# Front: mask products right behind their scores; slots 3 to 13: GpSimd's long operations behind the zero tests, moments ahead of the first matrix rows

## The chip, the cores and the metric

The kernel runs on one core of a Trainium2 chip. The metric is the device time of one execution in microseconds. The engines have short names in the views: PE is TensorE, DVE is VectorE, ACT is ScalarE, POOL is GpSimd, SP is SyncE, whose queue issues nearly all DMAs.

## The reference

```
def attention(decoder_output, encoder_output, mask):
    q = decoder_output @ wq_w + wq_b; k = encoder_output @ wk_w + wk_b; v = encoder_output @ wv_w + wv_b
    # 16 heads of 32
    score = einsum('bhqd,bhkd->bhqk', q, k) / sqrt(32)
    score = score * mask
    score = where(score == 0, -1e9, score)
    context = einsum('bhqk,bhkd->bhqd', softmax(score), v)
    return context @ wo_w + wo_b

def ffn(x):
    return real(ifft(fft(x) @ (w_freq_real + i w_freq_imag))) + bias

x = x + attention(layernorm(x), ctx_1024, mask)     # x is (2, 2048, 512), ctx_1024 is (2, 128, 512)
x = x + ffn(layernorm(x))
```

## The kernel before

The 4096 tokens are cut into 16 chunks of 256. A chunk takes four slots, one for each group of four heads, so there are 64 slots with scores (s = 4 * chunk + group), and the loop over v runs from 2 to 79, as later stages of a chunk trail its scores. Every engine has its own program, written out by hand in the order of the slots, and engines meet at semaphores alone. On each engine instructions start in program order, so one that waits holds everything behind it.

The stages of slot s, with the names of the code:

- PE `scores(s, t)` writes two score tiles into `scores`; it stands in the slot before (v = s - 1) and waits until the mask product of the slot before has read them.
- DVE `mask_mul(s)` (L917) multiplies the scores by the mask row scaled with the first layernorm's factor (`ms`), from PSUM into `zs`. DVE `zero_to_neg(s)` (L924, the zero test, which raises `eq_done`) turns exact zeros into the large negative value, in place in SBUF. DVE `least(s)` (L929) takes the minimum of each row and head.
- POOL `bias(s)` (L1151) scales that minimum into `nbias`, ACT `exps(s, t)` (L726) exponentiates, PE `turn(s, f)` transposes (L623), ACT `copy_pt` (L735) moves the result to SBUF, PE `weigh(m)` (L637) multiplies by the values for two slots at a time, and POOL `spread`, PE "R" and DVE `ctx_norm` normalise it.
- "WO" is the output projection with its residual, "FF" the folded frequency matrix, "Q" and "QQ" are query projections: "Q" of chunks 0 and 1 by quarters in the front, "QQ" of chunk c by halves, each 24 matmuls. `plan()` places the halves of chunk 2 in slots 2 and 4, those of chunk 3 in slots 5 and 6, and from slot 7 on one half in each odd slot.

PE's fp32-like products are made of fp16 pairs, a high and a low part. ACT `split_hi(c)` writes the high part `xth` of the transposed input, POOL `split_lo(c)` (L1102) the low part `xtl` and raises `p_l1`. A query projection of chunk c >= 1 waits for both:

```
                elif kind == "QQ":
                    pe.wait_ge(p_l1, c)
```

`xtl` and `xth` have two buffers, and the next `load_xt` on SP's queue waits for `p_l1` too. POOL's other long work is `fold(n)` (L1178, twelve additions that fold the frequency matrix; "U", which makes the matrix with "M", waits for six and then twelve of them), `low_o` (low part of the output weights), `add_bo` and `add_bf` (biases onto the residual, L1111 and L1137), `ctx_lo` (L1164), and `scale_mask(c)` (L1144). `stat_cols(c)` (L1088 to L1098) turns the moments of chunk c, which DVE makes with `stats1` and `mean1` (L955, L960), into columns that PE's "ST" transposes.

Before slot 2 stands the front, written out call by call on each engine. On PE it ends with S0 (scores of slot 0), W1, Q(0,2), Q(0,3), S1, ST1, Q(1,0), Q(1,1), S2, Q(1,2), Q(1,3). `scores(s)` of chunk 0 waits for `tt_done`, which `mask_mul` raises, and for the query quarter's low part.

In the loop POOL waits for `eq_done` of the same slot from slot VS = 9 on, ahead of its long operations. Below that slot it has no such wait.

Of the kernel before, what the change touches and what calls it, by code (L numbers as in the profile page):

```python
# [119 lines left out]
def bo_slot(c):  # L120

    return c + 7 if c < 3 else 4 * c + 3 if c < 13 else 2 * c + 27


def build(nc, x, xt, ctx_in, mask, wq, bq, wk, bk, wv, bv, wo, bo, lparts, tables, bf, eye, sums, pick, places, heads, out):
# [3 lines left out]
    with ExitStack() as stack:  # L129
# [213 lines left out]
        def _(sp):  # L343
# [87 lines left out]
            for v in range(V0, V1):  # L431
# [9 lines left out]
                if r == 0 and 5 <= c + 4 < NC:  # L441
                    load_xt(c + 4)
# [217 lines left out]
        def _(act):  # L660
# [172 lines left out]
        def _(dve):  # L833
# [190 lines left out]
            lo(at["Q", 1, 1])
            zero_to_neg(1)
            least(1)
            lo(at["Q", 1, 2])
            mask_mul(V0)
            lo(at["Q", 1, 3])
            for v in range(V0, V1):  # L1030
# [25 lines left out]
                for n in mids:  # L1056
                    if fills[n][0] == "M":
                        lo(n)
# [18 lines left out]
        def _(pool):  # L1077
# [150 lines left out]
            fold(3)
            for v in range(V0, V1):
# [3 lines left out]
                if v == VP:  # L1233
                    fold(7)
# [29 lines left out]
                if r < 2 and 0 <= c - 3 < NC:  # L1264
                    add_bf(c - 3, r)
# [16 lines left out]
                for a in (3, 4):  # L1282
                    if lo_slot(a) == v:
                        split_lo(a)
                if v == 3:
                    fold(6)
# [102 lines left out]
```

## Time and profile before

| | |
|---|---|
| median of 3 runs | 449.24 us (449.22 to 450.0) |
| profiled execution, its own time | 449.74 us |
| its span | 448.0 us |
| PE busy | 431.6 us, 96% |
| DVE busy | 402.7 us, 90% |
| ACT busy | 368.2 us, 82% |
| POOL busy | 361.0 us, 81% |

The span is what the profiler saw from the first to the last record; 1.74 us of the profiled execution's time lie around it. The busy time of an engine counts its data instructions alone. A row of the timeline gives start and duration in us, engine, source line, operation, and what it writes and reads. A bracket at its end is the idle time ahead of it and who ended that.

### The profile page before, as it was taken

To read this page: it belongs to the slowest core of one execution; us is meant where nothing else is said; L and a number is where in the kernel's file an instruction comes from. 1 tells how busy PE (TensorE), PEld (TensorE's weight loads), DVE (VectorE), ACT (ScalarE), POOL (GpSimd) and SP (SyncE) were. 2 spreads that over 40 slices of the span, in tenths; PEclk is the share of its full clock that TensorE was granted. 3 is DMA by queue.
4 is the path that set the end of the run, shared out by engine and by line. 5 is a ranking of instruction groups with operands and counts; after the bars stand their busy time and mean duration, and the time that the engine had idled before them with its cause. 6 is when DMAs were issued, how large, how long until landed. Compare 5 with 4: busy or idle time off the path is not lost.

```text
span 448.0 us, 10895 instructions
## 1 busy us (share of the span) xinstructions
PE 431.6 (96%) x3496; PEld 298.1 (67%) x3496; DVE 402.7 (90%) x532; ACT 368.2 (82%) x1342; POOL 361.0 (81%) x482
## 2 busy tenths in 40 slices
PE   7989999998899999999999999999999999989997
PEld 6877678786576666666776667666666765555444
DVE  3799899899999999999999999999999899999353
ACT  1648989799889989898989998989999899999620
POOL 5769997995779898989989898989898778755763
PEclk9999999999999999999999999999999999999999
DMA  8999754404434454545456554555442324431243
GB/s 271 397 385 221 249 190 113 129 1 119 113 105 93 136 126 119 148 117 139 128 139 137 129 145 113 121 104 130 137 95 64 97 75 96 78 83 35 61 115 121
DMA packets 85286, 60.15 MB, mean 134 GB/s; under 512 B 40141, under 2 KB 72813, under 8 KB 84718
## 3 DMA queue, kind: packets, MB, share of 16 engines
q1 hardware_dynamic: 84508, 59.29, 49.0%
q8 instruction: 29, 0.48, 0.5%
q14 instruction: 27, 0.22, 0.2%
q10 hardware_dynamic: 722, 0.17, 0.2%
HBM read 29.33 MB, written 8.39 MB: 84 GB/s over the span
## 4 chain that ended last, share of the span: by engine, by line
PE 68%; DVE 14%; issue 6%; ACT 5%; POOL 5%; DMA 1%; DVEq 0%; SPq 0%; POOLq 0%; ACTq 0%
PE bank L464 27%; PE bank L469 18%; PE bank L623 8%; PE bank L637 5%; DVE zs L924 4%; PE scores L609 4%; ACT zs L726 3%; DVE zs L917 3%; PE bank L570 2%; POOL cl L1164 2%; PE bank L551 1%; DVE nmin L929 1%; DMA cxs<-in_ctx 1%; PE scores L469 1%; DVE x L902 1%
## 5 line engine op out<-in xcount | busy, mean ns | idle before, releaser
L726 ACT ACTIVATE zs<-zs,nbias 128x128 f32<-128x128 f32 x512 | 199.5, 395 | 18.0 <-POOL nbias L1151 17.3
L726 ACT ACTIVATION_READ_ACCUMULATOR zs<-zs,nbias 128x1 f32 x512 | 98.4, 192 | 0.0
L924 DVE SCALAR_TENSOR_TENSOR zs<-zs 128x1024 f32<-128x1024 f32 x64 | 92.1, 1439 | 1.1
L929 DVE TENSOR_REDUCE nmin<-zs 128x8 f32<-128x1024 f32 x64 | 78.1, 1220 | 2.1
L917 DVE TENSOR_TENSOR zs<-scores,ms 128x1024 f32<-128x1024 f32 x64 | 78.0, 1219 | 0.1
L735 ACT COPY pt<-bank 128x512 f32<-128x512 f32 x128 | 67.8, 580 | 7.4 <-PE bank L623 7.3
L623 PE MATMUL bank<-ident,zs 128*128 128x128 f32 x512 | 67.0, 274 | 1.9 <-ACT zs L726 1.9
L1111 POOL TENSOR_TENSOR xs<-xs,bob 128x512 f32<-128x512 f32 (+1 forms) x41 | 42.8, 1048 | 24.7 <-DVE zs L924 21.6
L623 PEld LDWEIGHTS bank<-ident,zs 128*128 128x128 f32 x512 | 57.5, 140 | 5.6 <-ACT zs L726 4.5
L469 PE MATMUL bank<-xth,wqh 128*128 128x256 f16 x224 | 61.2, 273 | 0.0
L469 PE MATMUL bank<-xth,wql 128*128 128x256 f16 x224 | 61.1, 273 | 0.0
L469 PE MATMUL bank<-xtl,wqh 128*128 128x256 f16 x224 | 61.1, 273 | 0.0
L464 PE MATMUL bank<-woh,ch 128*128 128x512 f16 x128 | 48.5, 379 | 2.9 <-POOL cl L1164 2.1
L464 PE MATMUL bank<-woh,cl 128*128 128x512 f16 x128 | 48.5, 379 | 0.0
L464 PE MATMUL bank<-wol,ch 128*128 128x512 f16 x128 | 48.5, 379 | 0.0
L464 PE MATMUL bank<-mh,x1h 128*128 128x512 f16 x120 | 45.5, 379 | 0.0
L464 PE MATMUL bank<-ml,x1h 128*128 128x512 f16 x120 | 45.5, 379 | 0.0
L464 PE MATMUL bank<-mh,x1l 128*128 128x512 f16 x120 | 45.5, 379 | 0.0
L609 PEld LDWEIGHTS scores<-ks,qs 102*128 102x128 f16 (+1 forms) x480 | 31.7, 97 | 16.6 <-DVE zs L917 3.6
L1137 POOL TENSOR_TENSOR x<-x,bfb 128x512 f32<-128x512 f32 x32 | 40.8, 1276 | 0.0
L1164 POOL TENSOR_TENSOR cl<-cn,ch 128x512 f16<-128x512 f32 x32 | 38.1, 1190 | 3.3 <-ACT ch L749 3.3
L1158 POOL COPY rzb<-rz 128x512 f32<-128x512 f32 x32 | 40.6, 1268 | 0.2 <-DVE rz L935 0.2
(125 smaller groups left out, 910.8 us busy)
## 6 DMA issues: line engine op xcount, KB each, us to landing
xs<-in_x SPq DMA_DIRECT2D x16, 512.0 KB, 4.7
xtr<-in_xt SPq DMA_DIRECT2D x16, 512.0 KB, 4.4
out<-x SPq DMA_DIRECT2D x31, 256.0 KB, 2.5
qs<-qh SPq DMA_DIRECT2D x120, 64.0 KB
lp<-in_lparts SPq DMA_DIRECT2D x4, 1024.0 KB, 9.9
qs<-ql SPq DMA_DIRECT2D x60, 64.0 KB
ms<-in_mask SPq DMA_DIRECT2D x16, 128.0 KB, 2.4
wks<-in_wk SPq DMA_DIRECT2D x2, 512.0 KB, 6.8
```

The lines of the kernel that those rows point to most:

```text
L464: last = pe.matmul(o, a, b, start=(i == 0), stop=(i == len(mm) - 1))
L469: last = pe.matmul(o, a, b, start=(first and i == 0), stop=(i == len(pairs) - 1))
L609: last = pe.matmul(A[:, n % 2, 128 * j:128 * j + 128], qs[c % 2][0:rows, g, j, 128 * t:128 * t + 128], ks[0:rows, g, j, c // (NC // NB), : ...
L623: last = pe.transpose(PB[f][:, a:a + 128], zs[:, s % NZ, t, 2 * f + i, :], ident[:])
L726: last = act.activation(z, z, ACT.Exp, bias=nbias[:, s % 4, i:i + 1], scale=-NEG, accum_out=zsum[:, s % 4, i:i + 1])
L735: act.copy(pt[:, s % 2, 2 * f:2 * f + 2, :], PB[f][:]).then_inc(pt_copied, 1)
L917: dve.tensor_tensor(zs[:, s % NZ], A[:].rearrange("p t (h k) -> p t h k", h=4), ms[:, c % NM].unsqueeze(2).broadcast_to([128, 2, 4, KEYS]) ...
L924: dve.scalar_tensor_tensor(out=z, in0=z, scalar=0.0, in1=z, op0=ALU.is_equal, op1=ALU.subtract).then_inc(eq_done, 1)
L929: dve.tensor_reduce(nmin[:, s % 4, :], zs[:, s % NZ].rearrange("p t h k -> p (t h) k"), AX.X, ALU.min).then_inc(mn_done, 1)
L1111: i = pool.tensor_tensor(z, z, bob[:, n], ALU.add)
L1137: pool.tensor_tensor(z, z, bfb[:], ALU.add).then_inc(p_x1b, 1)
L1164: pool.tensor_tensor(cl[:, c % 2, 2 * h:2 * h + 2, :], cn[:], ch[:, c % 2, 2 * h:2 * h + 2, :], ALU.subtract).then_inc(p_cl, 1)
```

## The change

No instruction's size changes. What changes is the order on DVE and POOL, one pair of calls on ACT, and the place of one load on SP.

- Front, DVE: `mask_mul(0)` and `mask_mul(1)` move up; the moments of chunks 1 and 2 are pulled apart and stand around other work. Front, ACT: `exps(1, 0)` ahead of the copy of Q(1,3). Front, POOL: `bias(0)` between folds 0 and 1, then a wait for the second zero test, fold 2, `bias(1)`, and only then `split_lo(2)`.
- POOL's wait for the zero test starts at VP = 4. Folds 6 to 11 get new places (6 to 9 in slot 4, 10 and 11 in slot 5).
- `split_lo(3)` moves from slot 3 to slot 6, and `split_lo(4)` from slot 6 to slot 7, in halves around `bias`. `scale_mask(2)` moves from slot 4 to the end of slot 6, `add_bo(2, .)` from slot 9 to 10, `add_bf(0, 0)` from the middle of slot 12 to its end.
- The moments of chunk 6 move from slots 10 and 11 into slot 8, and the DVE part of "M" 0 goes behind them. `load_xt(5)` moves from slot 4 to slot 6 of SP's program.

```
--- before.py
+++ after.py
@@ -18,7 +18,6 @@
 NC = NB * S // CH
 NS = 4 * NC
 V0, V1 = 2, NS + 16
-VS = 9
 VP = 4
 VQ = 13
 LAST = ("FF", NC - 1, 1)
@@ -102,7 +101,7 @@
 
 
 def stats_slot(c, t):
-    return 4 if c == 4 else 4 * (c - 4) + 2 + t
+    return 4 if c == 4 else 8 if c == 6 else 4 * (c - 4) + 2 + t
 
 
 def small_slot(c):
@@ -113,13 +112,9 @@
     return 5 if c == 4 else 4 * (c - 3)
 
 
-def lo_slot(c):
-    return 3 if c == 3 else 6
-
-
 def bo_slot(c):
 
-    return c + 7 if c < 3 else 4 * c + 3 if c < 13 else 2 * c + 27
+    return c + 7 if c < 2 else 10 if c == 2 else 4 * c + 3 if c < 13 else 2 * c + 27
 
 
 def build(nc, x, xt, ctx_in, mask, wq, bq, wk, bk, wv, bv, wo, bo, lparts, tables, bf, eye, sums, pick, places, heads, out):
@@ -438,7 +433,9 @@
                     load_mask(c + 2)
                 if r == 0 and 0 <= c - 4 < NC:
                     store(c - 4, 1)
-                if r == 0 and 5 <= c + 4 < NC:
+                if v == 6:
+                    load_xt(5)
+                if r == 0 and 6 <= c + 4 < NC:
                     load_xt(c + 4)
                 if r == 3 and 0 <= c - 2 < NC - 1:
                     turn_x1n(c - 2, 0)
@@ -782,8 +779,8 @@
             hi(at["Q", 1, 1])
             exps(0, 1)
             hi(at["Q", 1, 2])
+            exps(1, 0)
             hi(at["Q", 1, 3])
-            exps(1, 0)
             exps(1, 1)
             for v in range(V0, V1):
                 c, r = divmod(v, 4)
@@ -1009,22 +1006,28 @@
             lo(at["Q", 0, 0])
             low_q(1)
             lo(at["Q", 0, 1])
-            moments(1)
+            mask_mul(0)
+            stats1(1, 0)
             lo(at["W1", 1])
-            mask_mul(0)
+            stats1(1, 1)
+            mean1(1, 0)
+            mean1(1, 1)
             spread_k(1)
+            zero_to_neg(0)
+            least(0)
+            mask_mul(1)
             lo(at["Q", 0, 2])
-            zero_to_neg(0)
             lo(at["Q", 0, 3])
-            least(0)
+            zero_to_neg(1)
             lo(at["ST", 1])
-            mask_mul(1)
+            least(1)
             lo(at["Q", 1, 0])
-            moments(2)
             lo(at["Q", 1, 1])
-            zero_to_neg(1)
-            least(1)
+            stats1(2, 0)
+            stats1(2, 1)
             lo(at["Q", 1, 2])
+            mean1(2, 0)
+            mean1(2, 1)
             mask_mul(V0)
             lo(at["Q", 1, 3])
             for v in range(V0, V1):
@@ -1054,7 +1057,7 @@
                 if 0 <= v - 9 < 4:
                     low_m(v - 9)
                 for n in mids:
-                    if fills[n][0] == "M":
+                    if fills[n][0] == "M" and v > 8:
                         lo(n)
                 tasks = []
                 tasks += [(stats1, mean1, a, t) for a in range(4, NC) for t in range(2) if stats_slot(a, t) == v]
@@ -1068,6 +1071,8 @@
                     recip((v - 3) // 2)
                 for _, mean, *ct in tasks:
                     mean(*ct)
+                if v == 8:
+                    lo(at["M", 0])
                 if c - 2 == NC - 1 and r < 2:
                     last_lo2(r)
                 if v == 2:
@@ -1218,20 +1223,19 @@
             split_lo(1)
             stat_cols(1)
             fold(0)
+            bias(0)
             fold(1)
-            bias(0)
+            pool.wait_ge(eq_done, 2)
+            fold(2)
+            bias(1)
             split_lo(2)
             stat_cols(2)
-            bias(1)
             scale_mask(1)
-            fold(2)
             fold(3)
             for v in range(V0, V1):
                 c, r = divmod(v, 4)
                 if v == 8:
                     constant_row()
-                if v == VP:
-                    fold(7)
                 for a in range(5, NC):
                     if small_slot(a) == v:
                         stat_cols(a)
@@ -1239,8 +1243,16 @@
                     rstd2(c - 2, 0)
                 if r == 2 and 0 <= c - 2 < NC:
                     rstd2(c - 2, 1)
-                if VS <= v < NS:
+                if VP <= v < NS:
                     pool.wait_ge(eq_done, v + 1)
+                if v == 4:
+                    fold(6)
+                if v == 5:
+                    fold(10)
+                if v == 6:
+                    split_lo(3, slice(0, 2), False)
+                if v == 7:
+                    split_lo(4, slice(0, 2), False)
                 for a in range(5, NC):
                     if v == 4 * a - 11:
                         split_lo(a, slice(0, 2), False)
@@ -1253,15 +1265,19 @@
                         add_bo(a, 1)
                 if 0 <= v < NS:
                     bias(v)
-                for n in {2: (4, 5), 4: (8, 9), 5: (10, 11)}.get(v, ()):
+                for n in {2: (4, 5), 4: (7, 8, 9), 5: (11,)}.get(v, ()):
                     fold(n)
+                if v == 6:
+                    split_lo(3, slice(2, 4))
+                if v == 7:
+                    split_lo(4, slice(2, 4))
                 if v % 2 == 1 and 0 <= v - 5 < NS:
                     ctx_lo((v - 5) // 2)
                 if r == 2 and 0 <= c - 2 < NC - 1:
                     norm_lo2(c - 2, 0)
                 if r == 3 and 0 <= c - 2 < NC - 1:
                     norm_lo2(c - 2, 1)
-                if r < 2 and 0 <= c - 3 < NC:
+                if r < 2 and 0 <= c - 3 < NC and v > 12:
                     add_bf(c - 3, r)
                 if v == 3:
                     low_o(0)
@@ -1279,15 +1295,14 @@
                         add_bo(a, 1, slice(0, D // 2), False)
                     if bo_slot(a) + 3 == v:
                         add_bo(a, 1, slice(D // 2, D))
-                for a in (3, 4):
-                    if lo_slot(a) == v:
-                        split_lo(a)
-                if v == 3:
-                    fold(6)
                 if v > VP and v % 2 == 1 and 0 <= v - 3 < NS:
                     spread((v - 3) // 2)
-                if r == 0 and 2 <= c + 1 < NC:
+                if v == 6:
+                    scale_mask(2)
+                if r == 0 and 3 <= c + 1 < NC:
                     scale_mask(c + 1)
+                if v == 12:
+                    add_bf(0, 0)
 
 
 def frequencies():
```

The order of POOL in slots 4 to 6 before, from the last fold ahead of `scale_mask(2)` to `spread(1)`; nbias rows are `bias` of slots 5 and 6:

```order
L1178 TENSOR_TENSOR lp<-lp 128x512 [waits d_lp3]
L1144 TENSOR_SCALAR ms<-ms,rs_99 128x128 [waits p_st,d_m2]
L1144 TENSOR_SCALAR ms<-ms,rs_99 128x128
L1151 TENSOR_SCALAR nbias<-nmin 128x8 [waits ex_done,mn_done]
L1178 TENSOR_TENSOR lp<-lp 128x512
L1178 TENSOR_TENSOR lp<-lp 128x512 [waits l_done]
L1164 TENSOR_TENSOR cl<-cn,ch 128x512 [waits ch_done]
L1158 COPY rzb<-rz 128x512 [waits g_done,rz_done]
L1151 TENSOR_SCALAR nbias<-nmin 128x8 [waits ex_done,mn_done]
```

The same slots of POOL in the changed kernel, from slot 5's wait on:

```order
L1183 TENSOR_TENSOR lp<-lp 128x512 [waits eq_done]
L1156 TENSOR_SCALAR nbias<-nmin 128x8 [waits ex_done,mn_done]
L1183 TENSOR_TENSOR lp<-lp 128x512 [waits l_done]
L1169 TENSOR_TENSOR cl<-cn,ch 128x512 [waits ch_done]
L1163 COPY rzb<-rz 128x512 [waits g_done,rz_done]
L1107 TENSOR_TENSOR xtl<-xtr,xth 128x512 [waits h1_done,eq_done]
L1156 TENSOR_SCALAR nbias<-nmin 128x8 [waits ex_done,mn_done]
L1107 TENSOR_TENSOR xtl<-xtr,xth 128x512 [waits h1_done]
```

The two halves of `split_lo(3)`, which stood in slot 3 as one operation, are now the first long work of slot 6 and its first half waits for the seventh zero test; the second half, which raises `p_l1`, also stands behind `bias(6)`.

PE's program in slot 5, from U 1 on, is the same in both; these are its rows of before, with the scores of slot 6, `weigh(1)`, and the first matmul of QQ(3,0):

```order
L469 MATMUL bank<-tb,lp 128x256 [waits d_tb,l_done,g_free]
L469 MATMUL bank<-tb,lp 128x256 x3
L609 MATMUL scores<-ks,qs_64 128x128 [waits tt_done]
L609 MATMUL scores<-ks,qs_64 128x128 x7
L637 MATMUL bank<-pt,vs 32x256 [waits cn_done,pt_copied]
L637 MATMUL bank<-pt,vs 32x256 x7
L469 MATMUL bank<-xth,wqh 128x256 [waits p_l1,g_free]
```

Nothing moved on PE: the projection that waits for `p_l1` of chunk 3 stays at the end of slot 5, so the work that it waits for now stands a slot later on POOL than the projection on PE.

DVE's front before, from the moments of chunk 1 to the second mask product:

```order
L955 BN_STATS st_96<-xs 128x6 [waits a1_done,d_x1]
L955 BN_STATS st_96<-xs 128x6 [waits a1_done]
L960 BN_AGGR ag_97<-st_96 128x2 [waits s1_done] x2
L869 TENSOR_TENSOR wz<-bank,wz 32x256 [waits g_hi]
L871 ISA [waits wz_lo]
L917 TENSOR_TENSOR zs<-scores,ms 128x1024 [waits p_ms,sc_done]
L978 COPY kbd<-kl 32x2x128 [waits g_free,p_kz]
L978 COPY kbd<-kl 32x2x128 x3
L886 TENSOR_TENSOR ql<-bank,qh 128x256 [waits g_hi]
L924 SCALAR_TENSOR_TENSOR zs<-zs 128x1024 [waits tt_done]
L886 TENSOR_TENSOR ql<-bank,qh 128x256 [waits g_hi]
L929 TENSOR_REDUCE nmin<-zs 128x8 [waits eq_done]
```

The same stretch of DVE in the changed kernel, to the low parts of Q(0,2) and Q(0,3):

```order
L914 TENSOR_TENSOR zs<-scores,ms 128x1024 [waits p_ms,sc_done]
L952 BN_STATS st_96<-xs 128x6 [waits a1_done,d_x1]
L866 TENSOR_TENSOR wz<-bank,wz 32x256 [waits g_hi]
L868 ISA [waits wz_lo]
L952 BN_STATS st_96<-xs 128x6 [waits a1_done]
L957 BN_AGGR ag_97<-st_96 128x2 [waits s1_done] x2
L975 COPY kbd<-kl 32x2x128 [waits g_free,p_kz]
L975 COPY kbd<-kl 32x2x128 x3
L921 SCALAR_TENSOR_TENSOR zs<-zs 128x1024 [waits tt_done]
L926 TENSOR_REDUCE nmin<-zs 128x8 [waits eq_done]
L914 TENSOR_TENSOR zs<-scores,ms 128x1024 [waits p_ms,sc_done]
L883 TENSOR_TENSOR ql<-bank,qh 128x256 [waits g_hi] x2
```

The first mask product went ahead of the moments, the moments' end (L957) behind it and behind W1, and the second mask product up by two query low parts and one "ST".

## Rows read from the trace of the kernel before

**Rows 1.** The page: busy time of PE, share of the span, instructions
```profile
PE 431.6 (96%) x3496; PEld 298.1 (67%) x3496; DVE 402.7 (90%) x532; ACT 368.2 (82%) x1342; POOL 361.0 (81%) x482
```

**Rows 2.** Windows: stretch, length, PE, PEld, DVE, ACT, POOL busy, clock, DMA, GB/s
```profile
150.00:350.00 200.00, 200.00 (x1684) 136.80 (x1682) 194.68 (x249) 183.59 (x685) 176.73 (x240) 1.00 0.49 122
```

**Rows 3.** Timeline of PE: all its idle times over 0.2 us, 17 to 350 us
```profile
31.81 0.23 PE L469 MATMUL scores<-kbd,qh 128*128 128x128 f16 x1 [1.88 <-DVE zs L917]
...
62.29 1.07 PE L637 MATMUL bank<-pt,vs 128*32 128x256 f32 x16 [0.41 <-ACT pt L735]
...
69.76 0.63 PE L570 MATMUL bank<-ident,rzb 128*128 128x128 f32 x4 [0.28 <-POOL rzb L1158]
...
102.78 0.62 PE L609 MATMUL scores<-ks,qs 102*128 102x128 f16 x8 [1.33 <-DVE zs L917]
...
116.54 0.62 PE L609 MATMUL scores<-ks,qs 102*128 102x128 f16 x8 [1.35 <-DVE zs L917]
```

**Rows 4.** Timeline of DVE, slots 4 to 6
```profile
52.38 1.22 DVE L917 TENSOR_TENSOR zs<-scores,ms 128x1024 f32<-128x1024 f32 x1
53.64 2.92 DVE L924 SCALAR_TENSOR_TENSOR zs<-zs 128x1024 f32<-128x1024 f32 x1
...
57.73 0.75 DVE L854 TENSOR_TENSOR us<-bank,od 128x256 f32<-128x256 f32 x2
...
59.81 1.23 DVE L917 TENSOR_TENSOR zs<-scores,ms 128x1024 f32<-128x1024 f32 x1
...
61.56 1.22 DVE L924 SCALAR_TENSOR_TENSOR zs<-zs 128x1024 f32<-128x1024 f32 x1
62.82 1.22 DVE L929 TENSOR_REDUCE nmin<-zs 128x8 f32<-128x1024 f32 x1
...
65.43 1.16 DVE L917 TENSOR_TENSOR zs<-scores,ms 128x1024 f32<-128x1024 f32 x1
```

**Rows 5.** Timeline of POOL: split_lo(3) whole, and a half of split_lo(5)
```profile
53.35 2.13 POOL L1102 TENSOR_TENSOR xtl<-xtr,xth 128x1024 f16<-128x1024 f32 x1
...
98.13 1.17 POOL L1102 TENSOR_TENSOR xtl<-xtr,xth 128x512 f16<-128x512 f32 x1
```

**Rows 6.** Timeline of PE, end of slot 5: scores of slot 6, QQ(3,0)
```profile
61.27 0.61 PE L609 MATMUL scores<-ks,qs 96*128 96x128 f16 x8
...
63.30 0.28 PE L469 MATMUL bank<-xth,wqh 128*128 128x256 f16 x1
```

**Rows 7.** Timeline of ACT: the copy of U 0
```profile
56.53 0.37 ACT L681 COPY od<-bank 128x256 f32<-128x256 f32 x1
```

**Rows 8.** Timeline of DVE, front
```profile
22.36 0.30 DVE L960 BATCH_NORM_AGGREGATE ag<-st 128x2 f32<-128x6 f32 x2
...
23.77 1.23 DVE L917 TENSOR_TENSOR zs<-scores,ms 128x1024 f32<-128x1024 f32 x1
24.91 2.01 DVE L978 COPY kbd<-kl 32x256 f16<-32x256 f16 x4
...
27.29 1.86 DVE L924 SCALAR_TENSOR_TENSOR zs<-zs 128x1024 f32<-128x1024 f32 x1
...
30.54 1.21 DVE L917 TENSOR_TENSOR zs<-scores,ms 128x1024 f32<-128x1024 f32 x1
```

**Rows 9.** Timeline of POOL, front: stat_cols(1), first and last operation
```profile
23.10 0.24 POOL L1088 TENSOR_SCALAR ve<-ag 128x2 f32<-128x2 f32 x1
...
25.40 0.20 POOL L1098 TENSOR_TENSOR stok<-ag,h 128x4 f16<-128x4 f32 x1
```

**Rows 10.** Timeline of PE: warm-up matmuls at the start, ST1
```profile
2.28 3.17 PE L643 MATMUL bank<-qh 128*128 128x256 f16 x14 [2.28 <-POOL srow L1208]
...
7.46 1.26 PE L643 MATMUL bank<-qh 128*128 128x256 f16 x10
...
26.81 0.28 PE L477 MATMUL bank<-ident,stok 128*128 128x128 f16 x2
```

**Rows 11.** Timeline of DVE, slot 12: the low part of M 3
```profile
112.82 1.69 DVE L908 SCALAR_TENSOR_TENSOR ml<-mf,mh 128x512 f16<-128x512 f32 x1
```

More of the change, by code:

```diff
@@ L440, in _ @@
                     store(c - 4, 1)
-                if r == 0 and 5 <= c + 4 < NC:
+                if v == 6:
+                    load_xt(5)
+                if r == 0 and 6 <= c + 4 < NC:
                     load_xt(c + 4)
@@ L1011, in _ @@
             lo(at["Q", 0, 1])
-            moments(1)
+            mask_mul(0)
+            stats1(1, 0)
             lo(at["W1", 1])
-            mask_mul(0)
+            stats1(1, 1)
+            mean1(1, 0)
+            mean1(1, 1)
             spread_k(1)
+            zero_to_neg(0)
+            least(0)
+            mask_mul(1)
             lo(at["Q", 0, 2])
-            zero_to_neg(0)
             lo(at["Q", 0, 3])
-            least(0)
+            zero_to_neg(1)
             lo(at["ST", 1])
-            mask_mul(1)
+            least(1)
             lo(at["Q", 1, 0])
-            moments(2)
             lo(at["Q", 1, 1])
-            zero_to_neg(1)
-            least(1)
+            stats1(2, 0)
+            stats1(2, 1)
             lo(at["Q", 1, 2])
+            mean1(2, 0)
+            mean1(2, 1)
             mask_mul(V0)
@@ L1056, in _ @@
                 for n in mids:
[L1057 removed]
+                    if fills[n][0] == "M" and v > 8:
                         lo(n)
@@ L1255, in _ @@
                     bias(v)
-                for n in {2: (4, 5), 4: (8, 9), 5: (10, 11)}.get(v, ()):
+                for n in {2: (4, 5), 4: (7, 8, 9), 5: (11,)}.get(v, ()):
                     fold(n)
+                if v == 6:
+                    split_lo(3, slice(2, 4))
+                if v == 7:
+                    split_lo(4, slice(2, 4))
                 if v % 2 == 1 and 0 <= v - 5 < NS:
@@ L1281, in _ @@
                         add_bo(a, 1, slice(D // 2, D))
[L1282 to L1286, printed above, removed]
                 if v > VP and v % 2 == 1 and 0 <= v - 3 < NS:
                     spread((v - 3) // 2)
-                if r == 0 and 2 <= c + 1 < NC:
+                if v == 6:
+                    scale_mask(2)
+                if r == 0 and 3 <= c + 1 < NC:
                     scale_mask(c + 1)
+                if v == 12:
+                    add_bf(0, 0)
 def frequencies():
```

32 lines of the change are left out of this document (19 added, 13 removed).

## Prediction

> **What bounds the kernel now.** I read the page first: PE is busy 96% of the span [rows 1]. That can hide waits, so I asked for stretches: from 150 to 350 us PE is busy 200.00 of 200.00 us, while DVE has 194.68 [rows 2]. The reader is to see that in the steady slots PE has no gap and DVE is 2.7% short of being the bound. The third view is PE's timeline with its idle times. Between 17 and 350 us there are five above 0.2 us, 5.25 us together [rows 3]: 1.88 at the scores of slot 2, 0.41 and 0.28 in slots 5 and 6, 1.33 and 1.35 at the scores of slots 12 and 14. Three of them, 4.56 us, wait for a mask product on DVE. So the kernel's time up to the last chunks is PE's own work plus those idle times. PE's work is not touched by the change. What the change does to the time is what it does to PE's idle time, one for one, as there is no slack later on PE to take up a loss. The most that better order can win ahead of 350 us is 5.25 us.
>
> Why DVE is late at those places is seen in its own timeline. The zero test of slot 4 takes 2.92 us [rows 4], that of slot 5 takes 1.22. The first starts at 53.64, while POOL runs a long subtraction from 53.35 to 55.48 [rows 5]; 55.48 plus 1.2 is about its end, 56.56. So a zero test that meets a long POOL operation waits until that is over. The low part of M 3 takes 1.69 us in the same way [rows 11], against an estimate of 0.7 for it alone. That is the loss that the new waits on POOL go after.
>
> **The change part by part.**
>
> Front. Before, the moments of chunk 1 end at 22.66 and POOL's six column operations run 23.10 to 25.60, 2.5 us [rows 8, 9]; PE takes them at ST1 at 26.81 without waiting [rows 10]. Now DVE does the mask product of slot 0 first (it can start when the scores end, an estimate of 21.5) and W1 between the moments: 1.15 for the product, 0.6, 0.5, 0.6 and 0.3 for the rest, with a short wait for W1's copy. The moments end near 24.7, the columns at 27.2 if POOL is free. It isn't: the four copies into `kbd` and the zero test of slot 0 now run beside them, and one of the two has to wait, up to 1.2 us. I take 28.2, so PE waits 1.4 us at ST1 where it waited none. Behind that PE has 3.1 us of work (26.81 to 31.81 less 1.88 [rows 3, 10]) and comes to the scores of slot 2 at 31.3. The second mask product, at 30.54 before [rows 8], now starts near 28.8 and ends near 30.0, with the low part of Q(0,2) 0.35 later: ready before PE comes. Scores 2 start at 31.3 to 31.4 in place of 31.81. **Front: -0.4** (ends: -1.4 with free columns, +0.6 with two blocks). The exponents of slots 0 and 1 come earlier on ACT, which nobody waits for here.
>
> Slot 4. The zero test no longer meets `split_lo(3)`, nor folds: DVE is 0.4 (front) plus 1.7 us earlier. But the copy of U 0 on ACT stands behind ACT's own exponents, ends at 56.90 [rows 7], and DVE's `us` (57.73 [rows 4]) needs it. With ACT 0.4 earlier DVE idles some 0.7 us there. The mask product of slot 5 comes at 58.6 in place of 59.81.
>
> Slot 5 to 6, the part that decides. `split_lo(3)` was done at 55.48, and PE began QQ(3,0) at 63.30 [rows 5, 6]: 7.8 us of cover. Now it stands in slot 6 of POOL behind the zero test of slot 6, while QQ(3,0) is still at the end of slot 5 of PE. From the rows of slot 5 [rows 4]: from mask product 5 to mask product 6 DVE takes 5.62 us (59.81 to 65.43), so product 6 is at 64.2. The zero test follows by 1.25 (52.38 to 53.64) and takes 1.25: 66.7, or 66.9 to 67.4 if it meets the end of `ctx_lo` or `spread(1)` on POOL. Then the first half of the split, 1.17 [rows 5]; `bias(6)` needs the minimum, 1.2 behind the zero test, and takes 0.25; then the second half, 1.17. Sum 2.65. `p_l1` reaches 3 at about 69.5. PE has done `weigh(1)` at 63.30 less 0.4 of the front and less the 0.41 that it idled there (ACT's copy is earlier by then): 62.5. **PE stands still for 7.0 us in slot 5** (ends: 3.9, if the mask product started at once when scores 6 end, 61.5, and 1.15, 1.25 and 2.5 follow; 7.7 with the collision). What is queued behind it on PE are the transposes of slot 4's exponents, U 2 and the scores of slot 7; ACT waits with its copy of the projection, DVE with the low part. So POOL's and DVE's gains in slots 6 to 8 can't be used: both wait for PE.
>
> Small idles. The two of slots 5 and 6 (0.41 and 0.28) vanish: **-0.7**. QQ(4,0) in slot 7 waits in the same way for `split_lo(4)`, now behind the zero test of slot 7. But PE has more between the scores of slot 7 and this projection (R 1, QQ(3,1), transposes, U 3, scores 8 and `weigh(2)`, an estimate of 7.5 us), against mask product, `ctx_norm`, zero test and the 2.65 on POOL, some 8 us with DVE's wait for U 2. **+0.4** (0 to 1.5).
>
> Slots 8 to 14. DVE saves the zero tests' stretches of slots 6 to 8, but it is waiting for PE anyway. The moments of chunk 6, 1.4 us, fall in slot 8, where DVE waits for PE's projection, and leave slots 10 and 11. DVE is then less late than PE, and the waits of 1.33 and 1.35 shrink. Not to nothing: `add_bo(2, .)`, two operations of 1.3 us, now runs in slot 10 beside the low part of M 1, and `add_bf(0, 0)` at the end of slot 12, near the low part of M 3, which it stretches today too. I leave 1.1 of 2.7: **-1.6** (ends -2.7 and 0). From slot 14 on the two orders are the same and PE is dense, so the sum stays as it is to the end. `load_xt(5)` waits for the same `p_l1` and is far ahead of its use (chunk 5's projection is in slot 11).
>
> Clock. An idle time of 7 us is longer than any in this trace. What PE does out of rest is seen at the start: the first 14 warm-up matmuls take 3.17 us, 0.22 apart, the ten at 7.46 take 1.26, 0.11 apart [rows 10], so PE runs at half rate, 1.2 of 2.4 GHz, for at least the first 3.2 us and at most from 2.28 to 7.46. After 1.88 us of idling no half rate is seen. 7 us is nearer to a start out of rest, so I take a fall as likely. At half rate for 3.2 to 5.2 us PE loses 1.6 to 2.6 us. **+2.0** (0 if the clock holds).
>
> The Trainium skill (TensorE: Matmul & The Clock Gate, "Part 1: The HAM clock gate") has the engine's clock drop to half when it was idle for long enough, and rise again under sustained work. By that rule the clock falls in slot 5; without it the sum would end 2.0 us lower. The rows at the start agree with it, while no row here shows a fall later on.
>
> Sum: -0.4 + 7.0 - 0.7 + 0.4 - 1.6 = +4.7, and with the clock +6.7. On the profiled execution's own time, 449.74, that is 456.4; that execution was 0.5 above the median of the runs, so on the median of 449.24 it is **455.9 us**.
>
> **The rivals.**
>
> 1. The clock holds: 449.24 + 4.7 = 453.9 us. For it: the 1.88 us idle time cost no rate, and the column of the granted clock shows 1.00 [rows 2]. Against it: the half rate of the start, after an idle time of unknown length.
>
> 2. Faster: DVE keeps up. The place is mask product 6. If the waits of slots 4 and 5 bring DVE so far ahead that it follows PE at once in slots 2, 6, 12 and 14, the stall is 3.9 us and all 5.25 us of old idles go: 449.24 - 1.3 = 447.9 us, clock unharmed. It decides from the point where `p_l1` comes less than 5.2 us after PE is ready, with no loss in the front. Against it: DVE would have to reach product 6 at 61.5, 2.7 us ahead of my working, while slot 4 is held by ACT's copy of U 0.
>
> 3. POOL becomes the bound behind the stall. In slots 7 and 8 it now has `split_lo(4)`, `ctx_lo(1)`, `add_bo(0)` and `add_bo(1)`, `spread(2)`, the constant row that M 0 needs, and the columns of chunk 5, all behind the zero test. If the constant row or `ctx_lo` is late, PE idles 1.5 us more: 457.4 us.
>
> 4. No change that can be told: the stall of about 4 us is just paid by the idles, clock held: 449.2 us.
>
> **How the numbers follow.** Chances: forecast with the fallen clock 0.52, rival 1 0.27, rival 3 0.12, rival 2 0.05, rival 4 0.04. Only rivals 2 and 4 end below 451, so the range starts at 452.0 (rival 1 with a better front and smaller idles, -1.9) and ends at 458.2 (rival 3 with the collision). What differs by less than 0.2%, 0.9 us, can't be told from no change here. Slower by more than that: the forecast and rivals 1 and 3, 0.91; within it 0.04; faster 0.05.
>
> **What would show it.** In the profile after: one idle time of PE of 6 to 7.7 us ahead of the first QQ(3,0) matmul, released by POOL's `xtl`; matmuls of the projection behind it 0.22 apart, not 0.11, for 3 to 5 us; PE's busy share down; ST1 waiting for POOL's columns by about a microsecond; zero tests of 1.22 to 1.3 us in slots 4 to 8; the scores of slots 12 and 14 with less idle time than 1.3 us each. I am wrong if PE starts QQ(3,0) before 66 us, if an idle time of PE has slack behind it that I did not see, or if PE's half rate lasts much longer than at the start.

## The result and the profile after

The changed kernel takes 455.88 us (median of 4 runs, 455.37 to 458.37), the kernel before on the same chip 449.36 us. The ratio is 1.0153 with a 95% interval of 1.013 to 1.0175: slower by 6.5 us. Forecast were 455.9 us and a range of 452.0 to 458.2. The profiled execution took 456.06 us.

The page after: span, busy time of each engine, the granted clock in 40 slices.

```profile
span 454.3 us, 10901 instructions
...
PE 432.7 (95%) x3496; PEld 298.7 (66%) x3496; DVE 398.8 (88%) x532; ACT 368.0 (81%) x1342; POOL 361.1 (80%) x484
...
PEclk9999987999999999999999999999999999999999
```

PE's busy time is nearly that of before [rows 1], DVE's is 3.9 us less, and the span is 6.3 us longer. (POOL has two instructions more, 484 in place of 482, as `split_lo(3)` and `split_lo(4)` are now two halves each.) DVE's work got shorter and the kernel got slower, and the clock row shows a dent in the sixth and seventh slice. PE's timeline after, its idle times above 0.2 us from 17 to 350 us and two matmuls of QQ(3,0), stands against [rows 3]:

```profile
19.41 0.22 PE L466 MATMUL scores<-kbd,qh 128*128 128x128 f16 x1 [0.41 <-DVE ql L883]
...
27.83 0.27 PE L474 MATMUL bank<-ident,stok 128*128 128x128 f16 x2 [1.38 <-POOL stok L1103]
...
68.81 0.37 PE L466 MATMUL bank<-xth,wqh 128*128 128x256 f16 x1 [7.14 <-POOL xtl L1107]
...
69.19 0.42 PE L466 MATMUL bank<-xtl,wqh 128*128 128x256 f16 x1
69.41 0.42 PE L466 MATMUL bank<-xth,wqh 128*128 128x256 f16 x1
...
84.84 0.27 PE L466 MATMUL bank<-xth,wqh 128*128 128x256 f16 x1 [0.57 <-POOL xtl L1107]
...
110.46 0.62 PE L606 MATMUL scores<-ks,qs 102*128 102x128 f16 x8 [1.18 <-DVE zs L914]
...
123.71 1.07 PE L634 MATMUL bank<-pt,vs 128*32 128x256 f32 x16 [0.38 <-ACT pt L732]
```

The third row is the stall: 7.14 us, released by POOL's second half of `split_lo(3)`. The two rows behind it start 0.22 apart. Before, the same two matmuls started 0.11 apart, and the next group of PE's program followed at 65.93:

```profile
63.53 0.27 PE L469 MATMUL bank<-xtl,wqh 128*128 128x256 f16 x1
63.64 0.27 PE L469 MATMUL bank<-xth,wqh 128*128 128x256 f16 x1
...
65.93 1.04 PE L623 MATMUL bank<-ident,zs 128*128 128x128 f32 x8
```

The windows around the stall after (columns as in [rows 2]):

```profile
62.00:64.00 2.00, 0.00 (x0) 0.00 (x0) 2.00 (x6) 2.00 (x9) 2.00 (x4) 0.94 0.02 6
64.00:66.00 2.00, 0.00 (x0) 0.00 (x0) 1.93 (x3) 0.03 (x1) 2.00 (x2) 0.50 0.44 103
66.00:68.00 2.00, 0.00 (x0) 0.00 (x0) 1.02 (x1) 0.00 (x0) 2.00 (x4) 0.50 0.46 107
...
70.00:72.00 2.00, 2.00 (x12) 1.36 (x10) 0.00 (x0) 0.00 (x0) 1.61 (x6) 0.50 0.32 77
...
76.00:78.00 2.00, 2.00 (x22) 1.76 (x21) 0.49 (x2) 1.84 (x9) 0.00 (x0) 1.00 0.01 2
```

PE has done nothing since 61.7, the clock falls to half (1.2 of 2.4 GHz) shortly before 64, and it is at half while the projection runs: 12 matmuls in 2 us. (The 22 of the last row, at full rate, are a mix of sizes; the like-for-like comparison is the projection itself.) Its 24 matmuls take 5.08 us, from 68.81 to the next group at 73.89, against 2.63 before, 63.30 [rows 6] to 65.93: 2.45 us are lost by rate alone.

DVE and POOL, slots 4 to 6, show why `p_l1` came when it did:

```profile
52.42 1.22 DVE L921 SCALAR_TENSOR_TENSOR zs<-zs 128x1024 f32<-128x1024 f32 x1
...
55.70 0.76 DVE L851 TENSOR_TENSOR us<-bank,od 128x256 f32<-128x256 f32 x2 [0.80 <-ACT od L678]
...
57.79 1.23 DVE L914 TENSOR_TENSOR zs<-scores,ms 128x1024 f32<-128x1024 f32 x1
...
63.35 1.16 DVE L914 TENSOR_TENSOR zs<-scores,ms 128x1024 f32<-128x1024 f32 x1
64.54 1.22 DVE L921 SCALAR_TENSOR_TENSOR zs<-zs 128x1024 f32<-128x1024 f32 x1
```

```profile
64.63 1.61 POOL L1163 COPY rzb<-rz 128x512 f32<-128x512 f32 x1
66.20 1.15 POOL L1107 TENSOR_TENSOR xtl<-xtr,xth 128x512 f16<-128x512 f32 x1
67.32 0.23 POOL L1156 TENSOR_SCALAR nbias<-nmin 128x8 f32<-128x8 f32 x1
67.52 1.15 POOL L1107 TENSOR_TENSOR xtl<-xtr,xth 128x512 f16<-128x512 f32 x1
```

The zero test of slot 4 is whole again, 1.22 in place of the 2.92 of [rows 4]. DVE loses 0.80 of that at the copy of U 0. `spread(1)` met the zero test of slot 6 and took 1.61 us, so the first half started 0.4 us after the zero test's end.

The traced executions differ ahead of the first score matmul, which starts between 19.21 and 21.85 us in them. So to compare them I count from there: the start of the last matmul is 425.01 us behind it before (19.93 to 444.94), and 431.86 after (19.41 to 451.27), +6.85. It is also the right measure for edits of a microsecond, and it is called the inner time below.

### The profile page after: what moved, and what is told of

Read it like the earlier page. It is cut to its first block, busy times and chain, and to the rows that moved or that the text cites. A ratio compares the mean times of both kernels' runs of the same rounds, so it can differ in the third digit from the quotient of the medians.

```text
span 454.3 us, 10901 instructions
## 1 busy us (share of the span) xinstructions
PE 432.7 (95%) x3496; PEld 298.7 (66%) x3496; DVE 398.8 (88%) x532; ACT 368.0 (81%) x1342; POOL 361.1 (80%) x484
## 4 chain that ended last, share of the span: by engine, by line
PE 67%; DVE 12%; ACT 7%; issue 6%; POOL 5%; DMA 2%; SPq 1%; DVEq 0%; POOLq 0%; ACTq 0%
PE bank L461 29%; PE bank L466 16%; PE bank L620 8%; PE bank L634 5%; ACT zs L723 4%; PE scores L606 4%; DVE zs L921 3%; PE bank L567 2%; DMA xtr<-in_xt 2%; DVE zs L914 2%; ACT pt L732 1%; PE bank L548 1%; POOL cl L1169 1%; DVE x L899 1%; PE scores L466 1%
## 5 line engine op out<-in xcount | busy, mean ns | idle before, releaser
L921 DVE SCALAR_TENSOR_TENSOR zs<-zs 128x1024 f32<-128x1024 f32 x64 | 89.4, 1396 | 1.1
L466 PE MATMUL bank<-xth,wqh 128*128 128x256 f16 x224 | 62.3, 278 | 7.7 <-POOL xtl L1107 7.7
L620 PE MATMUL bank<-ident,zs 128*128 128x128 f32 x512 | 66.9, 274 | 1.9 <-ACT zs L723 1.9
L466 PE MATMUL bank<-xth,wql 128*128 128x256 f16 x224 | 62.2, 278 | 0.0
L466 PE MATMUL bank<-xtl,wqh 128*128 128x256 f16 x224 | 62.2, 278 | 0.0
L1163 POOL COPY rzb<-rz 128x512 f32<-128x512 f32 x32 | 42.5, 1327 | 2.4 <-DVE rz L932 2.4
L1107 POOL TENSOR_TENSOR xtl<-xtr,xth 128x512 f16<-128x512 f32 (+1 forms) x28 | 34.5, 1232 | 11.0 <-DVE zs L921 11.0
```

The costliest lines, as they stand in the source:

```text
L466: last = pe.matmul(o, a, b, start=(first and i == 0), stop=(i == len(pairs) - 1))
L620: last = pe.transpose(PB[f][:, a:a + 128], zs[:, s % NZ, t, 2 * f + i, :], ident[:])
L921: dve.scalar_tensor_tensor(out=z, in0=z, scalar=0.0, in1=z, op0=ALU.is_equal, op1=ALU.subtract).then_inc(eq_done, 1)
L1163: pool.tensor_copy(rzb[:].rearrange("p i h w -> p (i h) w"), rz[:, z, :].rearrange("p i h -> p (i h)").unsqueeze(2).broadcast_to([128, 16, ...
```

## The experiments

**`split_lo(3)` back in slot 3.**

```
                     spread(0)
                     low_o(1)
+                    split_lo(3)
...
-                if v == 6:
-                    split_lo(3, slice(0, 2), False)
...
-                if v == 6:
-                    split_lo(3, slice(2, 4))
```

> The changed kernel with split_lo(3) back in slot 3, as one operation; all else as changed. Theory (the stall in slot 5 and the clock it costs are the whole loss): PE's idle time of 7.14 us ahead of QQ(3,0) and the 2.45 us of half rate behind it vanish; the zero test of slot 4 again meets the split (+1.7 on DVE, half of it hidden by ACT's copy of U 0), and the waits of the slots 12 and 14 come back in part: 446.5 to 449, so faster than the changed kernel by 7 to 9 us and faster than or like the kernel before. Rival (the waits behind zero tests cost by themselves, by late biases or folds): stays above 450.

Measured: 446.84 us (9 runs), ratio to before 0.9946 (0.9928 to 0.9963), inner time 422.66. PE at QQ(3,0), and the zero test of slot 4 on DVE:

```profile
68.34 0.28 PE L466 MATMUL bank<-xth,wqh 128*128 128x256 f16 x1 [0.53 <-DVE ql L886]
```

```profile
52.34 2.59 DVE L921 SCALAR_TENSOR_TENSOR zs<-zs 128x1024 f32<-128x1024 f32 x1
```

The stall and the half rate are gone: QQ(3,0) has no wait, and the row at 68.34 is QQ(3,1), with a small one. The zero test of slot 4 is stretched again to 2.59 us and that costs next to nothing. One line's place turns a loss of 6.5 us into a gain of 2.6. The other theory, that the waits cost by themselves, falls.

**That part alone on the kernel before.**

```
-                if VS <= v < NS:
+                if VS <= v < NS or v == 6:
                     pool.wait_ge(eq_done, v + 1)
+                if v == 6:
+                    split_lo(3, slice(0, 2), False)
...
+                if v == 6:
+                    split_lo(3, slice(2, 4))
```

`lo_slot(3)` is set out of reach, and `load_xt(5)` moves as in the change.

> The kernel before with one part of the change: split_lo(3) in slot 6, in halves around bias(6), behind the seventh zero test, with load_xt(5) moved to slot 6. Theory: this part alone makes the loss: one idle time of PE of 6 to 7.5 us in slot 5, half rate behind it, 454 to 457. Rival (it needs the other moves): under 452.

Measured: 459.11 us (4 runs), ratio 1.0212 (1.0176 to 1.0248), inner time 434.51. PE and POOL in slots 5 and 6:

```profile
71.39 0.37 PE L471 MATMUL bank<-xth,wqh 128*128 128x256 f16 x1 [8.48 <-POOL xtl L1104]
```

```profile
63.55 2.61 POOL L1180 TENSOR_TENSOR lp<-lp 128x512 f32<-128x512 f32 x2
66.12 2.13 POOL L1166 TENSOR_TENSOR cl<-cn,ch 128x512 f16<-128x512 f32 x1
68.20 0.61 POOL L1160 COPY rzb<-rz 128x512 f32<-128x512 f32 x1
68.77 1.15 POOL L1104 TENSOR_TENSOR xtl<-xtr,xth 128x512 f16<-128x512 f32 x1
```

The part alone makes the loss, and 2.1 us more than my upper end. Without the other moves both late folds stand behind `bias(5)`, `ctx_lo` meets the zero test and takes 2.13, and the split starts at 68.77. The stall is 8.48 us. So it was POOL's own queue, not the zero test, that ended last here.

**The stall kept, PE kept busy in it.**

```
                 elif kind == "QQ":
+                    if (c, f) == (3, 0):
+                        for i in range(60):
+                            pe.matmul(o[:, 0:256], wqh[:, 0, 0:128], wqh[:, 1, 0:256], start=True, stop=True)
                     pe.wait_ge(p_l1, c)
```

> The changed kernel with 60 matmuls of 128x256 on constant weights put into the bank of QQ(3,0) ahead of its wait; their result is overwritten by the projection. They fill 6.6 of the 7.14 us. Theory (the fall of the clock is a cost of its own): the projection's matmuls come 0.11 apart in place of 0.21, and the time falls by 2.0 to 2.6 us, to 453.3 to 453.9. Rival (what is lost by half rate would be idle time anyway, as DVE and ACT are late): within 0.7 us of the changed kernel.

Measured: 453.53 us (4 runs), ratio to before 1.0095 (1.0067 to 1.0123), inner time 429.38, 2.48 less than the changed kernel. PE and a window of it:

```profile
62.14 6.72 PE L556 MATMUL bank<-wqh 128*128 128x256 f16 x60
69.28 0.28 PE L466 MATMUL bank<-xth,wqh 128*128 128x256 f16 x1 [0.41 <-POOL xtl L1110]
```

```profile
70.00:72.00 2.00, 2.00 (x20) 1.81 (x19) 0.00 (x0) 0.00 (x0) 1.69 (x6) 1.00 0.31 73
```

The clock stays at 1.00, and 20 instead of 12 matmuls fit into 2 us. The projection starts as late as in the changed kernel (49.34 us behind the first scores, against 49.40) and the time is 2.35 us less. The fall of the clock is a cost of its own, 2.35 to 2.5 us of the 6.5, and here matmuls whose result is not used avoid it.

**The front alone on the kernel before.** All that the diff shows ahead of slot 2 on DVE, ACT and POOL:

```
             lo(at["Q", 0, 1])
-            moments(1)
+            mask_mul(0)
+            stats1(1, 0)
             lo(at["W1", 1])
-            mask_mul(0)
...
```

> The kernel before with the change's front alone (DVE, ACT and POOL ahead of slot 2). Theory: the wait of 1.88 us at the scores of slot 2 goes, one of about 1.4 comes at ST1; 0.4 to 0.5 us less: 448.8 to 449.0. Rival (the front's gain is real and lost later): 447.8 or less; rival (front costs): 449.8 or more.

Measured: 448.19 us (12 runs), ratio 0.9981 (0.9965 to 0.9997), inner time 423.97, 1.04 less than before. PE's idle times:

```profile
28.58 0.27 PE L477 MATMUL bank<-ident,stok 128*128 128x128 f16 x2 [1.39 <-POOL stok L1104]
...
61.50 1.07 PE L637 MATMUL bank<-pt,vs 128*32 128x256 f32 x16 [0.15 <-ACT pt L735]
...
101.97 0.62 PE L609 MATMUL scores<-ks,qs 102*128 102x128 f16 x8 [1.33 <-DVE zs L917]
```

As forecast, 1.88 at the scores of slot 2 became 1.39 at ST1. Beyond that the wait at `weigh(1)` for ACT falls from 0.41 to 0.15, and a small idle time at about 36 us goes. The gain in inner time is 0.5 to 0.6 us more than expected.

**A stall in between: `split_lo(3)` in slot 5.**

```
                 if v == 5:
-                    fold(10)
+                    split_lo(3, slice(0, 2), False)
...
+                if v == 5:
+                    split_lo(3, slice(2, 4))
+                    fold(10)
+                    fold(11)
```

> The changed kernel with split_lo(3) in halves in slot 5, behind the sixth zero test and around bias(5), ahead of folds 10 and 11. Theory: p_l1 comes at about 63.4 us of the span, PE is ready at about 61.5, so a stall of 1.8 to 2.2 us, and no half rate behind it: 447.5 to 449.0. Rival (any stall there brings the half rate): over 450.5.

Measured: 448.73 us (12 runs, 448.17 to 451.06), ratio 1.0002 (0.9982 to 1.0021), inner time 424.20.

```profile
63.70 0.27 PE L466 MATMUL bank<-xth,wqh 128*128 128x256 f16 x1 [1.94 <-POOL xtl L1107]
```

The stall is 1.94 us, the clock holds in the profiled execution, and the inner time is 1.54 over that with slot 3. Not in every execution: two of the twelve, 449.89 and 449.91 us, have a mean granted clock of 0.996, where the others have 1.000. With stalls of 0, 1.94 and 7.14 us the inner time is 422.66, 424.20 and 431.86: the first step costs less than its stall, as the wait of 0.53 at QQ(3,1) goes, the second 7.66 for 5.20 more, its difference of 2.46 being the half rate.

**`split_lo(3)` in slot 4, `split_lo(4)` in slot 6.** The version that the results pointed to: both splits early, both behind a zero test, fold 9 a slot later.

```
                 if v == 4:
-                    fold(6)
+                    split_lo(3, slice(0, 2), False)
                 if v == 5:
-                    fold(10)
+                    fold(9)
+                if v == 6:
+                    split_lo(4, slice(0, 2), False)
...
-                for n in {2: (4, 5), 4: (7, 8, 9), 5: (11,)}.get(v, ()):
+                for n in {2: (4, 5), 4: (6, 7, 8), 5: (10, 11)}.get(v, ()):
```

> The changed kernel with split_lo(3) in halves in slot 4 behind the fifth zero test, folds 6 to 8 behind it, fold 9 in slot 5, and split_lo(4) in slot 6 where split_lo(3) stood. Theory: neither projection waits and no zero test of slots 4 to 8 meets a split; beside the kernel with split_lo(3) in slot 3 the waits of 0.53 and 0.34 go: 446.0 to 446.8. Rival (folds now late for U 2 or colliding with the zero test of slot 5): 447.2 or more.

Measured: 446.89 us (7 runs), ratio 0.9946 (0.9925 to 0.9967), inner time 422.47. Neither projection waits, but in their place stand two other rows:

```profile
67.96 1.97 PE L466 MATMUL bank<-tb,lp 128*128 128x256 f32 x8 [0.24 <-issue]
...
70.65 0.63 PE L567 MATMUL bank<-ident,rzb 128*128 128x128 f32 x4 [0.28 <-POOL rzb L1163]
```

The twelfth fold and `spread(1)` are now what is late (the first row names no releaser, but POOL's last fold ends at 67.86, 0.1 us ahead of it): 0.87 us of waits became 0.52. My 446.0 to 446.8 was just missed; it is no better than slot 3 by anything that the runs can tell.

**The moments of chunk 1 first again, on top of that.**

```
-            mask_mul(0)
-            stats1(1, 0)
-            lo(at["W1", 1])
-            stats1(1, 1)
-            mean1(1, 0)
-            mean1(1, 1)
+            moments(1)
+            mask_mul(0)
+            lo(at["W1", 1])
```

> The previous kernel with the moments of chunk 1 back ahead of the first mask product, which keeps its place ahead of W1. Theory (the wait of 1.38 us at ST1 is the price of the late moments): ST1 doesn't wait, the second mask product is ready at PE's arrival; 0.7 to 1.4 us less than the previous kernel: 444.8 to 445.8. Rival (PE then waits for DVE at the scores of slot 2 or 12 instead): within 0.4 us of it.

Measured: 446.77 us (10 runs, 445.47 to 448.48), inner time 421.19, 1.28 less. ST1 waits no more; the only row ahead of slot 2 is this:

```profile
23.83 0.28 PE L551 MATMUL bank<-srow,wz 128*128 128x256 f16 x1 [0.18 <-DVE wz L866]
```

By the median alone the rival would hold, but the ten runs lay too wide for a difference of a microsecond, so the same kernel ran a second time:

> The kernel with the moments of chunk 1 first once more, as its ten runs lay between 445.5 and 448.5. Theory: 1.3 us less than with the moments late, as its trace shows between the first scores and the last matmul: 445.4 to 446.2. Rival: like it, 446.8.

445.59 us (6 runs, 445.35 to 446.21), ratio to before 0.9923 (0.9903 to 0.9943), inner time 421.22. That is the fastest kernel of this study, 3.4 us under the one before. What spread the first ten is not known. It was not half rate, as all ten have a granted clock of 1.00. It may be the stretch ahead of the first scores: the profiled execution of the previous kernel was the slowest of its seven, 449.11 against 446.89, with a clock of 1.00, an ordinary inner time (422.47), and first scores at 21.85, 1.7 to 2.6 us later than in most other traces.

**Slot 3's version without the waits of slots 4 to 8.**

```
-                if VP <= v < NS:
+                if 9 <= v < NS:
                     pool.wait_ge(eq_done, v + 1)
```

> The kernel with split_lo(3) back in slot 3, without POOL's waits for the zero tests of slots 4 to 8 (they start at slot 9 as before). Theory: zero tests of slots 6 to 8 take 0.2 to 0.7 us longer, the scores of slots 12 and 14 wait a little longer: 447.0 to 447.8, against 446.84. Rival (the waits cost as much as they win): 446.4 to 446.8.

Measured: 446.72 us (6 runs), ratio 0.9944, inner time 422.54 against 422.66. The rival is right: in this order of POOL the new waits do nothing for the time. The zero tests of slots 4 to 8 took the same times (2.62 against 2.59 in slot 4, 1.48 in both in slot 5, 1.22 in both in slot 7). It is POOL that changes. The first half of `split_lo(4)` in slot 7, with the wait and without it:

```profile
72.74 1.16 POOL L1107 TENSOR_TENSOR xtl<-xtr,xth 128x512 f16<-128x512 f32 x1 [1.29 <-DVE zs L921]
```

```profile
71.28 2.23 POOL L1107 TENSOR_TENSOR xtl<-xtr,xth 128x512 f16<-128x512 f32 x1
```

With the wait POOL idles 1.29 us and the operation takes 1.16. Without it the operation starts together with the zero test (71.27 to 72.49) and takes 2.23. Counted from the first scores it ends only 0.3 us earlier. So there the zero test was not what was held, and the wait had nothing to protect.

**What took the wait at the scores of slot 14.** Before, it is 1.35 us [rows 3]; after, it is gone, and 0.38 us stand at `weigh(6)` behind it. First `add_bf(0, 0)` back in the middle of slot 12:

> The kernel with split_lo(3) back in slot 3, and add_bf(0, 0) back in the middle of slot 12. Theory: the low part of M 3 takes 1.7 us again and PE's wait of 1.3 us at the scores of slot 14 comes back in place of 0.39 at weigh(6): 0.6 to 1.0 us more than 446.84. Rival (the moments of chunk 6 in slot 8 made that gain): no change.

Measured: 447.03 us (8 runs, 0.9953), inner time 422.63. No change: the low part of M 3 is not hit again. It ends at 112.0, and POOL's `add_bf(0, 0)` starts at 112.5.

```profile
111.32 0.68 DVE L905 SCALAR_TENSOR_TENSOR ml<-mf,mh 128x512 f16<-128x512 f32 x1
```

Then the moments of chunk 6 back in slots 10 and 11:

```
-    return 4 if c == 4 else 8 if c == 6 else 4 * (c - 4) + 2 + t
+    return 4 if c == 4 else 4 * (c - 4) + 2 + t
```

> The kernel with split_lo(3) back in slot 3, and the moments of chunk 6 back in slots 10 and 11. Theory (their move is what took PE's wait at the scores of slot 14, as add_bf's move did not): that wait comes back with 0.9 to 1.4 us, and the time rises by 0.7 to 1.1 us from 446.84. Rival (the folds' new places and the zero-test waits of slots 9 to 13 did it): no change.

Measured: 448.28 us (12 runs, 447.72 to 451.25), ratio 0.999 (0.9975 to 1.0005), 1.4 more than with the moments in slot 8, where 0.7 to 1.1 were expected. Five of the twelve have a mean granted clock of 0.996 (448.53 to 451.25 us); the median of the other seven is 447.90, 1.1 more. The place is not the expected one: PE waits at the scores of slot 12.

```profile
104.45 0.62 PE L606 MATMUL scores<-ks,qs 102*128 102x128 f16 x8 [2.04 <-DVE zs L914]
```

That is 0.85 more than with the moments in slot 8 (1.19). At the scores of slot 14 there is no wait, and the low part of M 3 takes 0.68 here too. But this trace can't settle slot 14: PE lost 1.6 us to half rate between the two places (told at the end), so DVE had that much more time. The mask product that the scores of slot 14 need ends at 117.47, and they start at 118.36. With the clock held PE would have come at about 116.7, and an estimate of its wait from these rows is 0.5 to 0.7 us. So shown is that `add_bf`'s move alone wins nothing, and that the moments' move into slot 8, where DVE waits for PE anyway, wins 0.85 us at slot 12 and about 1.1 in the time; its share at slot 14 is an estimate.

**The low part of M 1 kept clear of POOL.** On the fastest kernel:

```
-    return c + 7 if c < 2 else 10 if c == 2 else 4 * c + 3 if c < 13 else 2 * c + 27
+    return c + 7 if c < 3 else 4 * c + 3 if c < 13 else 2 * c + 27
...
                 if r == 2 and 0 <= c - 2 < NC - 1:
+                    if v == 10:
+                        pool.wait_ge(m_lo, 2)
                     norm_lo2(c - 2, 0)
```

> The kernel with split_lo(3) in slot 4 and the moments of chunk 1 first, and two more edits: add_bo(2, .) back in slot 9, and POOL waits in slot 10 for the low part of M 1 before it starts norm_lo2(0, 0). Theory: the low part of M 1 takes 0.7 in place of 1.5 us, and PE's wait at the scores of slot 12 falls from 1.18 to 0.3 to 0.6; 0.5 to 0.9 us less from the first scores to the last matmul (421.2 before that). Rival (something else holds the mask product of slot 11): the wait stays over 1.0.

Measured: 446.19 us (6 runs), ratio 0.9931 (0.9909 to 0.9953), inner time 421.48.

```profile
99.60 0.62 PE L606 MATMUL scores<-ks,qs 102*128 102x128 f16 x8 [0.37 <-DVE zs L914]
...
100.60 1.07 PE L634 MATMUL bank<-pt,vs 128*32 128x256 f32 x16 [0.38 <-ACT pt L732]
...
113.10 0.62 PE L606 MATMUL scores<-ks,qs 102*128 102x128 f16 x8 [0.47 <-DVE zs L914]
```

```profile
96.87 0.68 DVE L905 SCALAR_TENSOR_TENSOR ml<-mf,mh 128x512 f16<-128x512 f32 x1
```

The low part of M 1 did what was expected (0.68 us, and the wait at slot 12 down to 0.37), though the two edits were not run apart. The time did not: it is 0.6 us over the 445.59. 0.38 and 0.47 appeared at the next two places, while the 0.38 at `weigh(6)` went. The low part of M 2 now takes 1.43 in place of 0.68 us (103.16), beside POOL's `ctx_lo`. The gain of 0.81 us at slot 12 was given back within two slots.

## Why the prediction was right

Counted from the first score matmul, which starts half a microsecond earlier in the profiled execution after. "Lag" is how much later the same matmul of PE's program starts after than before:

| step | predicted | measured |
|---|---|---|
| front | -0.4 (wait at ST1 1.4) | scores 2 at 11.88, then 11.46: -0.42 (wait 1.38) |
| start of QQ(3,0) | +6.2, stall 7.0 | 43.37, then 49.40: +6.0, stall 7.14 |
| half rate behind it | +2.0 | +2.45 |
| small idles of slots 5, 6, 7 | -0.7 with the 0.41 at weigh(1), then +0.4 | the old two gone, 0.57 at QQ(4,0); lag 8.48 behind QQ(3,0), 8.37 at QQ(4,0) |
| waits of slots 12, 14 | -1.6 | idle times 2.68, then 1.56: -1.1; lag 7.00 at weigh(6): -1.4 |
| end | +6.7 | +6.85 |

- *PE's idle time decides, one for one.* Right, to about 0.15 us for each wait: with the 1.35 at the scores of slot 14 gone the lag falls by 1.51. From 150 to 350 us PE is busy 200.00 us of 200.00 after as before [rows 2], so nothing behind slot 14 took up the loss: it is +7.0 at `weigh(6)` of slot 15 and +6.85 at the end.
- *The stall.* Right in place, releaser and size, by its own steps: the mask product of slot 6 forecast for 64.2 started at 63.35, the first half for 66.9 to 67.4 at 66.20, `p_l1` for 69.5 at 68.7. All are early by about 0.8, and 0.5 of it is the start; PE was ready as much earlier (61.7 for 62.5), so the stall kept its size. The collision with `spread(1)` happened, on POOL's side. The experiments show the cause: without the move the loss is gone, with the move alone it is there.
- *The clock.* The step with a chance of little over a half. It came true, and the filled stall shows its price apart: 2.35 us in the time and 2.48 in the inner time. By the start's rows I put it at 2.0; it was 2.45.
- *The number.* 455.9 forecast and 455.88 measured agree better than the working does: the price of half rate was 0.45 too low and the small terms were off by 0.2 to 0.5, in both directions. That they cancel is luck.
- *Slot 4 wins little.* Right: DVE waits 0.80 us for the copy of U 0. More than right: with `split_lo(3)` in slot 3 the waits behind the zero tests of slots 4 to 8 win nothing at all.
- *Waits of slots 12 and 14.* The term was mis-sized by 0.2 to 0.5, and its parts were other than told. The wait at slot 12 stayed at 1.18. The moments' move wins 0.85 there, but the low part of M 1, 0.68 us before, now takes 1.49 (106.92 to 108.41): it meets POOL's `norm_lo2(0, 0)` (106.70 to 107.87), and `add_bo(2, .)` starts only at 107.83. The wait at slot 14 vanished altogether. What took it is not shown: neither `add_bf` nor the moments put back alone brought it back, the second in a trace with half rate just ahead of that place. That `add_bf(0, 0)` at the end of slot 12 would stretch the low part of M 3 was wrong, it took 0.68 us. The low part of M 1 before, and POOL and DVE after:

```profile
99.21 0.68 DVE L908 SCALAR_TENSOR_TENSOR ml<-mf,mh 128x512 f16<-128x512 f32 x1
```

```profile
106.70 1.17 POOL L1131 TENSOR_TENSOR x1nl<-x,x1nh 128x512 f16<-128x512 f32 x1
106.92 1.49 DVE L905 SCALAR_TENSOR_TENSOR ml<-mf,mh 128x512 f16<-128x512 f32 x1
```

- *Rival 1* (453.9, clock held) is what the filled stall comes to, 453.53, with the stall kept and the fall of the clock taken out. *Rival 3* (POOL the bound behind the stall) did not come: M 0 did not wait.

What stays open: why the first ten runs of the kernel with the moments first lay in 3 us, what took the wait at the scores of slot 14, and why the clock fell in some executions with a stall near 2 us and not in others.

## What to carry to other kernels

When a producer moves behind a new wait, find its consumer's place in the other engine's program first, and write down the cover: here 7.8 us, spent by moving the split three slots while PE's projection stayed where it was. An edit that makes one engine's operations shorter is worth what PE's idle time loses by it, and the same order with that one producer left early was 2.6 us faster than the kernel before. If PE must stand still for long, matmuls into a bank that is about to be overwritten can keep its clock: here 6.72 us of them in a stall of 7.14 delayed nothing and saved 2.35 us.

## What was not expected of the hardware

In the kernel with the moments of chunk 6 moved back, PE's clock fell behind an idle time of only 2.04 us (at 104.45). Two windows of that trace, below the one before them, which has the full rate:

```profile
104.00:106.00 2.00, 1.49 (x24) 0.95 (x24) 2.00 (x3) 2.00 (x10) 0.00 (x0) 1.00 0.57 147
106.00:108.00 2.00, 2.00 (x14) 1.36 (x11) 1.95 (x3) 0.93 (x3) 0.46 (x1) 0.55 0.67 210
108.00:110.00 2.00, 2.00 (x14) 1.46 (x12) 1.91 (x6) 1.65 (x8) 2.00 (x3) 0.60 0.23 47
```

The fall comes when PE is already at work again, and half rate lasts from about 106.2 to 109.6. Its price is 1.6 us: against the same kernel with the moments in slot 8 the lag is 0.83 at the scores of slot 12 and 2.45 behind the slow matmuls. That execution took 451.25 us where the median of the kernel is 448.28. The other part of its excess stands ahead of the first scores, which start at 21.79 us, about 2 us later than in most other traces.

It was not the only one. The mean granted clock of this execution is 0.996. Five of the twelve of this kernel have that, two of the twelve with the stall of 1.94 us in slot 5, and none of the 71 runs of the kernel before beside the experiments (0.999 or 1.000), whose longest idle time of PE there is 1.88 us [rows 3]. So a stall of two microseconds may or may not cost half rate in a given run, and it then costs some 1.5 us. It does not explain every spread: the kernel before ranges from 447.8 to 451.9 us at a clock of 1.00.
